# A graph-attention and expert kernel: the residual addition and the low halves of the split rows, on GpSimd or on VectorE

## The reference: what is computed

```python
x = x + gnn(layernorm(x), adj, W, a)          # softmax over the neighbours, 4 heads
x = x + ffn(layernorm(x), Wg, bg, W1, b1, W2, b2)
# gnn: h = x @ W;  e = leaky_relu(s1[:, None] + s2[None, :]);  e = -inf where adj == 0
#      out = softmax(e) @ h
# ffn: top 2 of (x @ Wg.T + bg), softmax over the two
#      out = sum over them of p * (relu(x @ W1[e].T + b1[e]) @ W2[e].T + b2[e])
```

## Time and profile before

| | |
|---|---|
| time, median of 3 runs | 633.05 us (630.92 to 635.54) |
| the profiled execution's own time | 634.19 us |
| its span in the profile | 632.3 us |
| granted TensorE clock, mean | 0.926 |
| VectorE busy | 527.3 us, 83% |
| TensorE busy | 480.3 us, 76% |
| ScalarE busy | 448.0 us, 71% |
| GpSimd busy | 431.3 us, 68% |

### The profile page before, as it was taken

How to read it: one execution, slowest core, us unless ns; L and a number is a source line. 1 busy time by engine, 2 the same in 40 slices (tenths; PEclk the granted TensorE clock), 3 DMA queues, 4 the chain that set the end, 5 groups by cost and what they waited for, 6 DMA issues and landing times.

```text
span 632.3 us, 22386 instructions
## 1 busy us (share of the span) xinstructions
PE 480.3 (76%) x7450; PEld 438.6 (69%) x7509; DVE 527.3 (83%) x1577; ACT 448.0 (71%) x908; POOL 431.3 (68%) x384
## 2 busy tenths in 40 slices
PE   0787888766797877988785775889999999999000
PEld 0576877766697877978784665778888888888000
DVE  4789898989999999999998796668887788877197
ACT  1584888877887888888823855578888888886164
POOL 2242347888888888888886687777777777777400
PEclk9997899889988999999986899899999999999655
DMA  9921222022222322321112235233333323321399
GB/s 320 399 92 62 69 69 77 28 93 94 56 71 98 103 98 95 98 94 36 33 40 69 65 100 140 81 82 91 87 92 92 89 80 88 87 80 51 109 368 321
DMA packets 60781, 67.93 MB, mean 107 GB/s; under 512 B 7266, under 2 KB 46317, under 8 KB 60416
## 3 DMA queue, kind: packets, MB, share of 16 engines
q1 hardware_dynamic: 41936, 44.31, 22.8%
q0 software_dynamic: 8816, 17.46, 8.3%
q10 hardware_dynamic: 9920, 4.73, 2.6%
HBM read 44.16 MB, written 23.22 MB: 107 GB/s over the span
## 4 chain that ended last, share of the span: by engine, by line
issue 33%; DVE 29%; POOL 16%; DMA 8%; PE 7%; ACT 5%; POOLq 1%; SPq 1%; DVEq 0%; ACTq 0%
POOL expert_out L519 11%; DVE edge L816 3%; DVE G L824 3%; DVE bs L719 3%; PE bank L1369 2%; POOL expert_rows L469 2%; DMA G<-in_L_ffn_W 2%; ACT xn L575 2%; DVE T L833 2%; DMA adji<-expert_out 2%; DVE mv L722 1%; PE bank L1360 1%; DVE sc L759 1%; DVE s L895 1%; DMA G<-expert_out 1%
## 5 line engine op out<-in xcount | busy, mean ns | idle before, releaser
L519 POOL DMA_INDIRECT expert_out<-late,bidx x142 | 165.5, 1165 | 47.9 <-issue 45.3
L469 POOL DMA_INDIRECT expert_rows<-rowt,idx x128 | 150.2, 1174 | 40.1 <-issue 33.1
L570 ACT ACTIVATE G<-bank,s2c 128x512 uint8<-128x512 f32 x256 | 153.7, 703 | 0.0
L673 ACT ACTIVATE late<-bank,b1s,sc 128x256 f32<-128x256 f32 x284 | 137.3, 563 | 13.7 <-PE bank L1543 12.9
L1369 PE MATMUL bank<-V,G 128*128 128x66 bf16 x3072 | 133.0, 199 | 4.6 <-issue 1.6
L1369 PEld LDWEIGHTS bank<-V,G 128*128 128x128 fp8e4 x3072 | 122.9, 101 | 9.4 <-issue 2.5
L1560 PE MATMUL bank<-W2h,G 128*128 x1704 | 107.6, 220 | 18.1 <-DVE late L1239 16.7
L1560 PEld LDWEIGHTS bank<-W2h,G 128*128 128x128 f16 x1704 | 97.5, 98 | 34.1 <-issue 34.1
L1543 PE MATMUL bank<-late,W1h 128*128 128x256 f16 x852 | 107.2, 277 | 0.0
L1224 DVE TENSOR_TENSOR G<-late,G 128x1024 f16<-128x1024 f32 x71 | 87.0, 1226 | 2.4
L1543 PEld LDWEIGHTS bank<-late,W1h 128*128 x852 | 81.9, 100 | 9.1
(11 more groups left out here) (168 smaller groups left out, 747.6 us busy)
## 6 DMA issues: line engine op xcount, KB each, us to landing
adji<-in_adj SPq DMA_DIRECT2D x16, 1024.0 KB
V<-expert_rows SPq DMA_DIRECT2D x71, 130.0 KB
adji<-expert_out SPq DMA_DIRECT2D x8, 512.0 KB, 5.5
G<-expert_out SPq DMA_DIRECT2D x8, 512.0 KB, 7.7
expert_out<-late,bidx POOLq DMA_INDIRECT x142
G<-in_L_ffn_W SPq DMA_DIRECT2D x1, 2048.0 KB, 13.3
late<-in_L_ffn_W SPq DMA_DIRECT2D x1, 2048.0 KB, 9.8
expert_rows<-rowt,idx POOLq DMA_INDIRECT x128
```

The lines of the kernel that those rows point to most:

```text
L469: pool.indirect_dma_start(xs, bass.IndirectOffsetOnAxis(ap=idx[:, Z.q, k, j:j + 1], axis=0), rowt[:, Z.q, j, :], None).then_inc(scattered[ ...
L519: pool.indirect_dma_start(ybuf, bass.IndirectOffsetOnAxis(ap=bidx[:, B.o, t:t + 1], axis=0), ysb[:, B.q, t, :], None, bounds_check=2 * TOK ...
L570: act.activation(Gs[:, M.p, h // 2, mt, :, h % 2], zb[h][:, :], ACT.Sign, bias=s2c[:, M.p, mt, h:h + 1]).then_inc(S["z_used"], 1)
L673: act.activation(h32[:, U.p, c, :], Up[U.p][c // 2][:, (c % 2) * BLK:(c % 2 + 1) * BLK], ACT.Relu, bias=b1s[:, bass.ds(ex * NC + c, 1)], s ...
```

## The change

One number is changed:

```diff
-TAIL = NB - 2
+TAIL = 0
```

## The result

The changed kernel took 624.49 us (median of 6 runs, 622.89 to 626.30), beside 635.28 us for the kernel before in the same runs (630.92 to 636.23). The ratio is 0.9846 with a 95% interval of 0.9821 to 0.9872: it is about 1.5% faster, some 10 us. The forecast was 624.0 us.

What follows compares the result with a forecast made beforehand. VectorE was taken as the bound, part of its busy time being waits for GpSimd. With 20.6 us added, 22.1 and up to 8.4 gone, 9.9 less, cut to 9, gave 624 us; eight in ten from 616 to 639.

Steps and rivals of the forecast that it cites:

- VectorE bounds, and its busy time holds waits: Attention part: VectorE sets the pace, busy 287.56 of 307 us, but part of that is standing still for GpSimd.
- Added work, 20.6 us: On VectorE: 28 additions at 0.45 us (12.6 us) and 14 remainders at 0.57 us (8.0 us), with nothing hiding them.
- Stops that go directly, 22.1 us: VectorE operations stretched beside the moved GpSimd steps: 12.8 us beside L475 and 9.3 us beside L482 would go.
- indirectly, up to 8.4 us: Earlier L459 and a less delayed GpSimd queue: 3.3 us at L816, up to 3.6 at two small operations, 1.5 waiting for L437.
- the low end of the range: Forecast time 617 to 630 us, lower if remaining stretches, some 5 us beside scatters and L459, go too; eight-in-ten range from 616.
- The slots: Attention part: middle slots 17.9 instead of 18.04 us, those from 97 to 182 us up to 3 less, last three about 1 less.
- the late mask: L816 in the last three slots before 312 us, stretched by a late L459: 1.1 us less each, 3.3 us.
- the 9 us: Whole kernel's net gain: 9.9 us less, minus 1 us for new encounters; 624 us against the median of 633.05.
- Another engine taking the gain: Rival: L459 stops other operations or TensorE holds the slot, so indirect gains are lost; 631.5 us, chance 0.26.
- New stops beside scatters: Rival: the 42 added VectorE operations meet GpSimd's scatters, up to 23 us; 637 to 655 us, chance 0.14.
- The rule of the busiest engine: Read plainly, more work on VectorE costs the added 20.6 us, 654 us, at the end of the slower rival's range (0.14).
- the price of 0.56 us each: Assumed cost of each added VectorE operation that meets a scatter, up to 23 us for all 42.

Runs made afterwards that it cites:

- rows_twice: The changed kernel with the rows' remainder computed twice on VectorE, the first time into an area nobody reads: 633.95 us.
- rows_memset: The kernel before, with GpSimd filling the rows' low halves with zeros instead of subtracting, nothing put on VectorE: ratio 0.982 to the kernel before, 623.34 us.
- low_part_dve: The changed kernel with V's second piece (L459) moved from GpSimd to VectorE too, behind the edge mask: 639.67 us.
- rows_only: The kernel before with only the rows' remainder (L475) moved to VectorE, the additions staying on GpSimd for the first fourteen graphs: 625.81 us.
- add_late_again: The changed kernel with the addition one routing operation later, statistics where they were, timed a second time: 621.23 us, ratio 0.979 to the kernel before.

## Why the prediction was right

**VectorE bounds, and its busy time holds waits.** Shown: work added to it is paid in full (rows_twice, 0.59 us of time for 0.60 of work), and stops that are taken away are gained, with nothing put on in return (rows_memset, 11 us; 9.5 of 15.4 us of stretch in the attention part).

**Added work, 20.6 us.** Shown in its size: 0.46 us from L852 to L858 and 32 rows at 0.424 to 0.478 us, 0.60 us from L863 to the next where I had taken 0.57 from one place in the tail. With the measured prices it is 21.3 us.

**Stops that go directly, 22.1 us, and indirectly, up to 8.4 us.** Together 30.5 were forecast; the stretch fell by 31.7 us and the idle time by 1.4. The account then gives 31.7 + 1.4 - 20.6 = 12.5 us (11.8 with 21.3 us added), and the attention part was 11.8 us shorter. What came on top of the 30.5 is about the 2.9 us of stretches that ended with scatters: none is left in the trace after. The sum had them at nothing and named them only for the low end of the range. The division was less good. The remainder alone took away 20.1 us of stretch and not 12.8, and the additions alone 20.0 and not 9.3 and part of 8.4: the two overlap, since a late queue on GpSimd comes from both. What each is worth by itself (8 and 5 us) adds up to more than the 10 of both.

**The slots.** 17.9 us in the middle were forecast and 17.88 came; the late mask is 1.75 us where 1.8 was worked out, and the last slots are 1.25 us shorter each where about 1 was. "Up to 3 us less each" from 97 to 182 us holds for the stretch from 140 us (3.0), but between starts of L816 one slot gives 5.9 us, the one behind it is 1.0 longer, and those up to 143 us together give nothing.

**The number.** That it came out within 0.5 us (624.0 and 624.49) is in part luck. The attention part gained more than forecast (11.8 for 9), and 2 us of it didn't reach the end. And the 9 us were taken from a median of three runs, 633.05; with three more runs the kernel before has 635.28, so the measured gain is 10.8 us by the medians and 9.8 by the ratio. The gain was forecast somewhat too small, from a base somewhat too low.

**The rivals.** Another engine taking the gain: TensorE's waits for T went from 30.4 to 26.3 us, so VectorE was still ahead. New stops beside scatters: the median of the 32 L858 is 0.425 us and the longest 0.478, though 14 of them start while a scatter has 0.15 to 0.88 us to go (those take 0.424 to 0.426), and no L974, L977 or L980 stands in the account, so the price of 0.56 us each was never paid. The rule of the busiest engine (the Trainium skill, Perfetto Trace Analysis, "Identifying the Most-Contended Engine") named the right engine; the reading that it must not get more work failed, since its busy time in the attention part had 35.8 us of stretches in it.

The Trainium skill, Perfetto Trace Analysis, section "Optimizing Scalar/DVE Operations", says that moving work between VectorE and GpSimd might not help because they share a port. By that rule, the runs agree for one step and not for the other: low_part_dve puts 1.17 us of work in the place of 0.26 us of stops and is slower, and rows_only puts 0.60 in the place of 1.4 and is faster.

## What to carry to other kernels

A busy engine isn't an engine at work: compare an operation's duration with the shortest of the same form, and look on GpSimd's timeline for what ends when the long one ends. Moving a step from GpSimd to a saturated VectorE pays if its price there (from start to start) is below the stops that it causes, which is so here for L475, beside which an operation stood still in every slot, and not for L459, much of which runs beside operations that it doesn't stop (L719 and L722). Once it is moved, order is worth as much again: an operation that doesn't care between a result and its reader, and those that aren't stopped beside the GpSimd operation that remains, gave another 7.7 us by the medians.

## What the runs showed of the hardware

GpSimd's operations stopped VectorE operations with one SBUF input too, not only with two: the copy L941 took 0.47 for 0.19 us beside an L482, and the mask's L816, with an integer input, 2.93 for 1.20 beside L459. The 4x4 L913 (0.39 for 0.21 beside an L482) reads a tile and one value per partition, both in SBUF.

Not stopped in the kernel before, though they started while one of the three steps ran: the norm's statistics L719 (29 times; never over 0.296 us, with 0.259 the shortest) and L722 (26 times), the reduction L966 (8 times, 0.19 us at most), and operations of which an input lies in PSUM: the copy L891 (8 times inside L475, just ahead of the L895 that stops), L833 and L939.

With a fill of 0.54 us in the place of the subtraction of 1.17 us, an operation with two SBUF inputs that starts inside it takes 0.19 us as when alone (rows_memset).

A wait of VectorE for its own last result costs 0.12 us from start to start: 0.46 us from L852 to the addition that needs it, 0.34 us from L852 to an operation that doesn't (add_late_again).

And one chip ran the kernel before in 724 us, 14% longer than the others, with a granted clock of 0.87 to 0.89 in the profiles of the two kernels run there, where the others have 0.92 to 0.94; what that chip lacked I didn't find out.
